# Norm and logits of both routing heads in one block by groups of tokens; parameter rows spread by DMA; read-back and output moved into the experts' block

## The reference, cut to what matters

```python
x = x + 0.5 * _L0_ffn_ref(_layernorm(x), gate_w, w1, w2, w3)
x = x + _L0_attn_ref(_layernorm(x), W_qkvz, W_ba, conv_weight, A_log, dt_bias, norm_weight, W_out)
x = x + 0.5 * _L0_ffn_ref(_layernorm(x), gate_w, w1, w2, w3)
...
router_logits = x_flat @ gate_w                    # 2048 x 8
topk_w, topk_idx = top_k(softmax(router_logits), 2)
h = silu(rows @ w1[e]) * (rows @ w3[e]); out = h @ w2[e]      # rows sorted by expert
...
b, a = split(x @ W_ba)
g = -exp(A_log) * softplus(a + dt_bias); beta = sigmoid(b)
```

## Time and profile before

| | us |
|---|---|
| median of 3 runs | 3072.45 (3071.95 to 3075.09) |
| span of the profiled execution, first to last instruction | 3065.9 |
| PE busy | 2722.1 (89%) |
| DVE busy | 1929.4 (63%) |
| ACT busy | 1384.1 (45%) |
| POOL busy | 703.5 (23%) |

### The profile page before, as it was taken

The page is one execution under the profiler, slowest core; times in us unless marked ns, Lnnn a source line. Parts: engine busy times, 40 slices in busy tenths (PEclk is TensorE's granted clock), DMA queues, the critical chain, the costliest instruction groups (busy, mean ns, idle before and its releaser), DMA issues. The chain is left out here.

```text
span 3065.9 us, 58355 instructions
## 1 busy us (share of the span) xinstructions
PE 2722.1 (89%) x19346; PEld 2007.4 (65%) x19347; DVE 1929.4 (63%) x3648; ACT 1384.1 (45%) x4441; POOL 703.5 (23%) x954
## 2 busy tenths in 40 slices
PE   4999994556999999999999999999999995699996
PEld 4566663333677777777777777777777775566664
DVE  4122222588889889888898898898887543322221
ACT  0111111334666666666666666666665552111111
POOL 1222221322222222222221322213221111122221
PEclk7999996778999999999999999999999997699998
DMA  4223311345654544544545455455553321223322
GB/s 156 60 64 99 96 26 48 103 144 154 182 160 152 167 149 151 179 135 158 166 134 181 137 159 165 148 167 155 154 155 108 104 68 55 88 61 99 98 62 45
DMA packets 378125, 374.75 MB, mean 122 GB/s; under 512 B 213076, under 2 KB 293460, under 8 KB 377876
## 3 DMA queue, kind: packets, MB, share of 16 engines
q1 hardware_dynamic: 362900, 351.05, 36.4%
q0 software_dynamic: 14976, 20.46, 4.0%
HBM read 234.83 MB, written 138.67 MB: 122 GB/s over the span
## 5 line engine op out<-in xcount | busy, mean ns | idle before, releaser
L533 PE MATMUL f_ps_up<-f_wbuf,f_xgT 128*128 x1248 | 500.4, 544 | 5.4 <-issue 3.3
L628 DVE TENSOR_TENSOR f_h<-f_h,f_ps_up 128x448 f32<-128x448 f32 x156 | 96.9, 621 | 472.7 <-ACT f_h L602 472.7
L602 ACT ACTIVATE f_h<-f_ps_up 128x448 f32<-128x448 f32 x156 | 84.9, 544 | 636.3 <-PE f_ps_up L533 636.3
L533 PEld LDWEIGHTS f_ps_up<-f_wbuf,f_xgT 128*128 128x128 f32 x1248 | 231.7, 192 | 190.0 <-issue 185.3
L1265 PE MATMUL at_bank<-xnT,at_w_qk 128*128 128x512 f32 x512 | 273.6, 663 | 58.9 <-DVE at_qk L1589 55.5
L1589 DVE SCALAR_TENSOR_TENSOR at_qk<-at_bank,at_taps_qk,at_qk 128x510 f32<-128x510 f32 (+2 forms) x384 | 280.7, 744 | 46.2 <-ACT at_qk L1463 37.1
L1589 DVE SCALAR_TENSOR_TENSOR at_vT<-at_bank,at_taps_v,at_vT 128x510 f32<-128x510 f32 (+2 forms) x384 | 280.4, 744 | 36.0 <-ACT at_vT L1470 26.9
L1849 POOL TENSOR_SCALAR at_small<-at_small 128x4 f32<-128x4 f32 x64 | 17.4, 272 | 1215.1 <-ACT at_squares L1497 1215.1
L1443 PE MATMUL at_bank<-at_w_out,at_yT 128*128 128x256 f32 x1024 | 259.7, 402 | 36.2 <-issue 35.4
L500 POOL DMA_INDIRECT sums<-f_y,f_row_of x78 | 123.9, 1588 | 583.3 <-DVE f_y L639 583.3
L1290 PE MATMUL at_bank<-at_w_vz,xnT 128*128 128x256 f32 x1024 | 245.3, 383 | 9.0 <-DVE at_vT L1589 9.0
(11 more groups left out here) (233 smaller groups left out, 5607.8 us busy)
## 6 DMA issues: line engine op xcount, KB each, us to landing
f_wbuf<-in_L_ffn_w_dram SPq DMA_DIRECT2D x48, 896.0 KB, 7.0
at_steps_e<-steps_kept SPq DMA_DIRECT2D x64, 512.0 KB, 6.7
pt_kept<-at_pt_made SPq DMA_DIRECT2D x64, 512.0 KB, 2.7
mt_kept<-at_mt_made SPq DMA_DIRECT2D x64, 512.0 KB, 4.3
at_mt<-mt_kept SPq DMA_DIRECT2D x64, 512.0 KB, 4.1
at_pt<-pt_kept SPq DMA_DIRECT2D x64, 512.0 KB, 4.6
qk_kept<-at_qk SPq DMA_DIRECT2D x64, 256.0 KB, 2.6
ks_kept<-at_ks_made SPq DMA_DIRECT2D x64, 256.0 KB, 2.7
```

The lines of the kernel that those rows point to most:

```text
L533: last = te.matmul(ps_up[hf][w][:, 0:MH], xgT[b][:, k, :], wbuf[:, bass.ds(off + (w * WSIZE + k * M + hf * MH), MH)], start=(k == 0), stop ...
L628: v.tensor_tensor(part, part, ps_up[hf][1][:, 0:MH], ALU.mult).then_inc(h_ready, 1)
```

## The change

1. x is loaded in four DMAs, one for each group; POOL no longer waits for x in the constants' block.
2. `build_norm` is gone. Its work stands in the routing block: DVE does `moments(group)` and `shift(group - 1)`, POOL 1/std by groups of 4 tiles, PE `turn(group)` and `project(group - 1)`, ACT copies both halves. SP loads the gate and expert 0 first, then (in the first routing) waits for x, stores x to `sums`, and stores `xn` to `rows_in` by groups.
3. `A_log` and `dt_bias` are written to all partitions by two DMAs that read one row 128 times; POOL's spreading is gone.
4. SP waits in the experts' block for the last stores to `sums` and then issues the read-back of x (first part) or the output (second part). The output's own block is gone.

```diff
 build_constants
-            sp.dma_start(x[:], x_dram.rearrange("b (c p) d -> p (b c) d", p=P)).then_inc(c["x_loaded"], 16)
+            for group in range(4):
+                part = slice(4 * group, 4 * group + 4)
+                sp.dma_start(x[:, part, :], rows[:, part, :]).then_inc(c["x_loaded"][group], 16)
...
-            pool.wait_ge(c["x_loaded"], 16)
 build_ffn, routing: SP
-                    sp.dma_start(rows_in.rearrange("(t p) d -> p t d", p=P), xn[:]).then_inc(rows_stored, 16)
+                    if first:
+                        for group in range(4):
+                            sp.wait_ge(c["x_loaded"][group], 16)
                     sp.dma_start(sums[0:T, :].rearrange("(t p) d -> p t d", p=P), x[:]).then_inc(sums_begun, 16)
                     sp.dma_start(sums[T:T + P, :], c["zeros"][:]).then_inc(sums_begun, 16)
+                    for group in range(4):
+                        sp.wait_ge(xn_ready, 4 * group + 4)
+                        sp.dma_start(rows_in[512 * group:512 * group + 512, :].rearrange("(t p) d -> p t d", p=P),
+                                     xn[:, 4 * group:4 * group + 4, :]).then_inc(rows_stored, 16)
                     weight_loads(sp, 1, w1, w2, w3, wbuf, loaded)
 build_ffn, routing: PE
+                    def turn(group):
+                        pe.wait_ge(xn_ready, 4 * group + 4)
+                        at_least(pe, copied, 2 * (group - 1))
...
+                    def project(group):
+                        pe.wait_ge(gate_loaded, 16)
+                        pe.wait_ge(copied, 2 * group + 2)
...
+                    for group in range(4):
+                        turn(group)
+                        if group:
+                            project(group - 1)
+                    project(3)
 build_ffn, routing: DVE (POOL makes 1/std of 4 tiles at a time)
+                    def moments(group):
+                        if first:
+                            dve.wait_ge(c["x_loaded"][group], 16)
...
+                    for group in range(4):
+                        moments(group)
+                        if group:
+                            shift(group - 1)
+                    shift(3)
...
-                    dve.wait_ge(logits_done, 1)
+                    dve.wait_ge(logits_done, 4)
 build_ffn, experts: SP
+                    for b in range(RING):
+                        sp.wait_ge(rows_stored[b], 16 * GROUPS)
+                    if out is None:
+                        for group in range(4):
+                            rows = sums[512 * group:512 * group + 512, :]
+                            sp.dma_start(x[:, 4 * group:4 * group + 4, :], rows.rearrange("(t p) d -> p t d", p=P)).then_inc(c["x_back"][group], 16)
+                    else:
+                        sp.dma_start(out.rearrange("b (c p) d -> (b c) p d", p=P).rearrange("t p d -> p t d"),
+                                     sums[0:T, :].rearrange("(t p) d -> p t d", p=P)).then_inc(c["out_stored"], 16)
+                        sp.wait_ge(c["out_stored"], 16)
 attention_front
-                sp.dma_start(rows[:, 0, :], A_log.rearrange("(a n) -> a n", a=1)).then_inc(loaded, 16)
-                sp.dma_start(rows[:, 1, :], dt_bias.rearrange("(a n) -> a n", a=1)).then_inc(loaded, 16)
+                for n, row in enumerate((A_log, dt_bias)):
+                    sp.dma_start(row_all[:, n, :], row.rearrange("(a n) -> a n", a=1).to_broadcast([P, NV])).then_inc(rows_loaded, 16)
...
-                pool.wait_ge(loaded, 48)
-                nc.gpsimd.partition_broadcast(row_all[:].rearrange("p a n -> p (a n)"),
-                                              rows[:].rearrange("p a n -> p (a n)"), P).then_inc(spread, 1)
...
-                act.wait_ge(spread, 1)
+                act.wait_ge(rows_loaded, 32)
...
-                dve.wait_ge(spread, 1)
+                dve.wait_ge(rows_loaded, 32)
```

More of the change, by code:

```diff
@@ L140, in _ @@
             pool.wait_ge(made, n[0])
-            pool.wait_ge(made, n[0])
-            pool.wait_ge(c["x_loaded"], 16)
[L146 to L201, removed]
@@ L210, in weight_loads, with build_ffn @@
         eng.dma_start(dst.rearrange("p (k m) -> p k m", k=src.shape[1]), src).then_inc(loaded[e % 2], 16)
-def build_ffn(nc, c, x, xnT, gate_w, w1, w2, w3, rows_in, sums, prefix, first):
+def build_ffn(nc, c, x, xnT, gate_w, w1, w2, w3, rows_in, sums, prefix, first, out):
     ctx = ExitStack()
@@ L315, in _ @@
                 def _(act):
+                    for group in range(4):
+                        for k in range(KD):
+                            act.wait_ge(turned_ready, 2 * group + k + 1)
+                            nc.scalar.copy(xnT[:, k, 512 * group:512 * group + 512], turned[group % 2][k][:]).then_inc(copied, 1)
                     act.wait_ge(shifted, 1)
@@ L429, in _ @@
                 def _(pool):
+                    for group in range(4):
+                        part = slice(4 * group, 4 * group + 4)
+                        pool.wait_ge(moments_done, 4 * group + 4)
+                        nc.gpsimd.tensor_scalar(rstd[:, part], mv[:, part, 1], LN_EPS, None, ALU.add).then_inc(rstd_done, 1)
+                        pool.wait_ge(rstd_done, 2 * group + 1)
+                        nc.gpsimd.tensor_tensor(rstd[:, part], rstd[:, part], c["minus_half"][:, part], ALU.pow).then_inc(rstd_done, 1)
                     nc.gpsimd.iota(columns_i[:], [[1, P]], base=0, channel_multiplier=0).then_inc(numbers_made, 1)
@@ L655, in _, with build @@
                     copy_y(GROUPS - 1, RING - 1)
-def build_out(nc, c, sums, out):
-    with nc.Block() as block:
-        @block.sync
-        def _(sp):
-            sp.dma_start(out.rearrange("b (c p) d -> (b c) p d", p=P).rearrange("t p d -> p t d"),
-                         sums[0:T, :].rearrange("(t p) d -> p t d", p=P)).then_inc(c["out_stored"], 16)
-            sp.wait_ge(c["out_stored"], 16)
-def build(nc, x_in, W_qkvz, W_ba, conv_weight, A_log, dt_bias, norm_weight, W_out, gate_w, w1, w2, w3, out,
-          parts=("ffn", "attention", "ffn")):
+def build(nc, x_in, W_qkvz, W_ba, conv_weight, A_log, dt_bias, norm_weight, W_out, gate_w, w1, w2, w3, out):
     ctx = ExitStack()
@@ L680, in build @@
             ("zeros", [P, D], F32), ("iota_i", [P, TILES + 1], I32), ("iota", [P, TILES + 1], F32))}
-        for name in ("x_loaded", "constants_made", "out_stored"):
+        for name in ("constants_made", "out_stored"):
             c[name] = r.dma_sem(name)
+        for name in ("x_loaded", "x_back"):
+            c[name] = [r.dma_sem(f"{name}{group}") for group in range(4)]
         c["experts_loaded"] = {f"f{n}_": [r.dma_sem(f"f{n}_experts_loaded{k}") for k in range(2)] for n in range(2)}
@@ L726, in attention_front @@
         g_turned, rows_exp, rows_ready = q.sem("g_turned"), q.sem("rows_exp"), q.sem("rows_ready")
-        x_back = [q.dma_sem(f"x_back{k}") for k in range(4)] if pending is not None else []
         stats_done, moments_done = q.sem("stats_done"), q.sem("moments_done")
@@ L778, in project @@
                 def project(group):
[L779 removed]
+                    pe.wait_ge(loaded, 16)
                     pe.wait_ge(copied, 2 * group + 2)
@@ L838, in moments @@
                     part = range(4 * group, 4 * group + 4)
-                    if pending is not None:
-                        dve.wait_ge(x_back[group], 16)
+                    dve.wait_ge(c["x_back"][group], 16)
                     for t in part:
```

68 lines of the change are left out of this document (40 added, 28 removed).

## The result

| | before | after |
|---|---|---|
| median | 3073.77 us (3071.95 to 3076.40, 4 runs) | 3025.90 us (3023.84 to 3027.76, 4 runs) |
| ratio | | 0.9847, 95% interval 0.9833 to 0.9861 |
| span of the profiled execution | 3065.9 us | 3023.9 us (its own time 3025.58) |

The change makes the kernel 1.5% faster: 47.9 us by the medians, 42.0 by the two profiled spans. The forecast was 3029.3 us, with 43.2 us off the span.

The account below looks back on a forecast made before the run. Engines were taken to wait for one another, each doing all 16 tiles first. Savings 11.1 + 16.0 + 9.5 + 6.6 = 43.2 us cut the span from 3065.9 to 3022.7; adding 6.55 gave 3029.3 us, range 3021 to 3038.

Parts of the forecast that it names:

- First routing, -11.1: First routing: x and norm by groups end the logits at 31.0 instead of 42.14, 11.1 us less.
- The lower level throughout: First routing's transposes and logits: PE's clock taken as 0.50 (1.2 GHz) all the way, 21.4 us from first transpose.
- Attention's front, -16.0: Attention's front: earlier read-back and no POOL stall start shift(0) at 493.5 instead of 509.51, 16.0 us less.
- The choice on POOL's stall: Attention's front: POOL's unexplained 7.57 us before 1/std taken to go away with the spreading.
- Second routing, -9.5: Second routing: norm and logits by groups end the logits at 2599.5 instead of 2609.05, 9.5 us less.
- End, -6.6: Kernel's end: output leaves before POOL's drain and the clearing, span ends at 3059.3 instead of 3065.9, 6.6 us less.
- 6.55 us lie around the span: Whole kernel: median 3072.45 less profiled span 3065.9, added back to the new span to get the time.
- From about 500.4 on, each us of delay is one on the path: Attention's front: parameter rows landing after about 500.4, when ACT wants them, would lengthen the path us for us.
- fourth rival: Attention's front: parameter rows land late and hold up ACT, PE and DVE; 65 us after issue gives 3085; chance 0.03.
- The clock did not rise during the logits of 8 columns: Rival for both routings: clock rises during the new logits, 3023.5, or 3015.5 if up all the time; chance 0.10.
- The early transfers did not stay behind the drain: Rival at the experts' blocks' ends: early read-back and output still wait for POOL's drain, 3037.6 us; chance 0.06.
- the stall did not stay: Rival in the attention's front: POOL's stall stays, 7.6 us of the gain lost, 3036.9 us; chance 0.05.

Follow-up runs that it names:

- the two runs with the spreading: Kernel after with POOL again spreading the parameter rows, ahead of the first 1/std or behind the last: ratios 0.9901 and 0.9848 to the kernel before.
- the spreading last: Kernel after with POOL again spreading the parameter rows, behind the four 1/std: ratio 0.9848 to the kernel before.
- the three together: Kernel after with semaphores cleared by ranges, a drain ahead of the last three stores, and logits of 64 columns: 3004.25 us, ratio 0.9787 to the kernel before.

## Why the prediction was right, and where not

1. **First routing, -11.1.** Right, -11.0 at the logits' end and -11.4 at the gather. Every step on the path came within about 0.1: x at 4.93 (4.85), shift at 8.20 (8.1), first transpose at 9.63 (9.6), logits' end at 31.11 (31.0). The block began at 3.5 and not at 3.9, and waited for x. The lower level throughout was the right choice.
2. **Attention's front, -16.0.** Right in kind, -18.2 in the rows. Shift and first transpose came as worked out; the other 2.2 us are luck, since the clock rose during the second projection here and one projection later in the front before (2.41 instead of 3.51), and this varies from one execution to the next. The choice on POOL's stall was right, as the two runs with the spreading show. The second projection, before and after:

```profile
520.59 3.51 PE L783 MATMUL tab_ps_ba<-tab_w_ba,xnT 128*128 128x64 f32 x16
```

```profile
493.03 2.41 PE L772 MATMUL tab_ps_ba<-tab_w_ba,xnT 128*128 128x64 f32 x16
```

3. **Second routing, -9.5.** Right, -9.5.
4. **End, -6.6.** Right, -6.8; undone together with the read-back it costs 11.2.
5. **"6.55 us lie around the span."** This step failed. 1.7 us lie around it in every run whose span is known; by that the profiled execution of the kernel before was one of about 3067.6 us (3065.9 + 1.7), and the other 4.85 are its distance from the median. From profiled execution to profiled execution the sum gives 3022.7 + 1.7 = 3024.4, where the kernel after took 3025.58. That they agree to 1.2 us is in part luck: the edited stages saved about 46 us and not 43.2, and the attention came out 4.8 longer. From median to median the step did no harm: the forecast of 3029.3 is 3.4 above the measured 3025.90, about what the edited stages and the experts saved beyond the sum.
6. **"From about 500.4 on, each us of delay is one on the path"** (fourth rival). This failed too: ACT there has about 5 us of cover. The prediction has PE wait for ACT's copies before `turn(3)`; but `turn(3)` asks for the copies of the first two groups, which stand ahead of ACT's wait for the rows, and only the third projection asks for the ones behind it. With the spreading last, PE went through the second projection and the fourth transposes while ACT waited 5.3 us, and stood for 0.54. It did not decide, since the rows landed 3.0 and 3.9 us after their issue at 479.05 and 479.56, and ACT asks for them at 490.16 (DMA issues of the kernel after: count, KB each, median us to landing):

```profile
tab_row_all<-in_L_attn_A_log_dram SPq DMA_DIRECT2D x1, 16.0 KB, 3.0
tab_row_all<-in_L_attn_dt_bias_dram SPq DMA_DIRECT2D x1, 16.0 KB, 3.9
```

The rivals. The clock did not rise during the logits of 8 columns: in the second routing the granted clock was 0.50; with 64 columns in the same order it was 1.00 from 2557 on. The Trainium skill (TensorE: Matmul & The Clock Gate, Part 4: PE-mode transpose) was set against this rival, for the reason that transposes do not engage the full clock. The kernel before contradicts that reason more plainly than the 0.99 of the earlier trace rows, which stands mostly for a stretch without matmuls. Its second routing has only transposes on PE, behind 18.35 us of idleness:

```profile
2584.85 3.95 PE L193 MATMUL f_turned<-ident,f_xn 128*128 128x128 f32 x20 [18.35 <-DVE f_xn L180]
2589.33 1.53 PE L193 MATMUL f_turned<-ident,f_xn 128*128 128x128 f32 x12 [0.53 <-DVE xnT L184]
```

The last 12 take 1.53 us, that is 1.02 for eight, where eight take 1.97 at the lower level; the granted clock is 0.50 from 2580 to 2583 and 1.00 from 2589 to 2592. So the rival was rightly kept, and what decided against it was the logits behind them.

The early transfers did not stay behind the drain (469.58 and 3012.74, ahead of it both times), and the stall did not stay. x was little slowed by the weights behind it: its last quarter had landed by 9.60, when SP's store of x leaves, and the sum has 9.0.

## What to carry to other kernels

Where engines wait for one another over all tiles, cut the stage into groups and take the time from a stage of the same kernel that already runs so: nearly the whole error of that copy was the clock. Then look at what stands between the stages with nobody at work: here a drain cost 6.42 us, one clearing instruction per semaphore 5.0 behind the attention (77 fewer of them), and the change of POOL's configuration 5.70 to 7.57. And judge a few us by the rows of their stage, with several profiles of the same kernel beside them.

## What the runs showed of the hardware that I had not expected

- A POOL drain is paid for the gathers and stores since the drain before: 6.42 us behind 78, 0.29 behind 3, 0.04 to 0.05 behind none. Placed where POOL is idle, it cost the kernel nothing.
- The width of a matmul can cost less than nothing: a group's eight matmuls took 3.42 us with 8 columns, at a granted clock of 0.50, and 1.92 with 64 in the same place, at 1.00. It is not sure to: in the three together, the first two projections of the second routing took 3.52 each with 64 columns too.
- POOL stalled 5.70 us on the way into the spreading as well as 6.90 to 7.57 on the way out of it.
- Transposes alone ran at the upper level of the clock in the kernel before (12 in 1.53 us).
- The granted clock of these profiles can't be read for the first routing: there it shows 1.00, while eight transposes take 1.97 us, as they do at 0.50 in the second. Two stretches of the kernel after, by the same columns as above:

```profile
14.00:18.50 4.50, 4.50 (x24) 4.50 (x23) 2.96 (x12) 0.81 (x2) 2.24 (x6) 1.00 1.10 367
...
2558.00:2563.00 5.00, 5.00 (x26) 5.00 (x25) 2.35 (x10) 1.16 (x3) 1.82 (x5) 0.50 1.09 386
```

So the level in the first routing is read here from the durations.
